# A bounded number of gathers in flight in place of a full drain on the gather engine

## The reference

```
x = x + _L0_conv_ref(_gn(x), W, b)                 # attention over pixels, squared-ReLU scores
x = x + _L1_conv_ref(_gn(x), offset_w, ...)        # deformable convolution, 9 taps
x = x + _L2_conv_ref(_gn(x), w_i2s, ...)           # diagonal LSTM, two directions
x = x + _L3_conv_ref(_gn(x), w_conv, w_p, ...)     # deformable convolution with adaptive reach
```

```
sampled = (hh*hw) * gather(y0, x0)   + (hh*lw) * gather(y0, x0+1)
        + (lh*hw) * gather(y0+1, x0) + (lh*lw) * gather(y0+1, x0+1)
out = einsum('nckhw,ock->nohw', sampled * mask, wk)
```

## Time and profile before

| What | Value |
|---|---|
| median of three runs | 12763.94 us |
| span of the profiled execution | 13258.5 us |
| POOL busy | 7518.9 us (57%) |
| PE busy | 7451.2 us (56%) |
| DVE busy | 6180.1 us (47%) |
| ACT busy | 4757.6 us (36%) |
| mean granted TensorE clock | 0.745 of full speed |
| first stage, first to last gather | 465.7 to 6534.7 us |
| last stage, first to last gather | 8067.3 to 13235.7 us |
| moved by DMA | 1280.23 MB, of them 925.30 MB by the gathers |

### The profile page before, as it was taken

The page is one execution under the profiler, slowest core; times in us unless marked ns, Lnnn a source line. Parts: engine busy times, 40 slices in busy tenths (PEclk is TensorE's granted clock), DMA queues, the critical chain, the costliest instruction groups (busy, mean ns, idle before and its releaser), DMA issues. The chain is left out here.

```text
span 13258.5 us, 114790 instructions
## 1 busy us (share of the span) xinstructions
PE 7451.2 (56%) x29878; PEld 2708.4 (20%) x29878; DVE 6180.1 (47%) x8631; ACT 4757.6 (36%) x7391; POOL 7518.9 (57%) x7857
## 2 busy tenths in 40 slices
PE   7786776778777676853289992333232323233332
PEld 2222222222222222221123321111111111111111
DVE  1344444444433444445456664454455445545444
ACT  7664554646555454641156661111111111111100
POOL 0375655657565564757500004777777767767776
PEclk9897887889888787876599995565565656555665
DMA  0232232223322222337633337343434343433332
GB/s 9 66 96 87 85 93 80 87 89 96 92 85 79 89 85 86 91 94 172 164 86 81 82 78 139 101 121 101 120 97 119 101 111 98 120 97 101 100 96 90
DMA packets 1169072, 1280.23 MB, mean 97 GB/s; under 512 B 795966, under 2 KB 924414, under 8 KB 1164670
## 3 DMA queue, kind: packets, MB, share of 16 engines
q0 software_dynamic: 338688, 925.30, 23.5%
q1 hardware_dynamic: 815710, 347.84, 11.1%
q10 hardware_dynamic: 14368, 3.21, 0.1%
HBM read 1080.00 MB, written 195.82 MB: 96 GB/s over the span
## 5 line engine op out<-in xcount | busy, mean ns | idle before, releaser
L423 POOL DMA_INDIRECT b_gathered<-table,b_iu x3528 | 3701.6, 1049 | 1929.9 <-issue 1013.0
L423 POOL DMA_INDIRECT d_gathered<-table,d_iu x3528 | 3705.2, 1050 | 1420.4 <-issue 1041.0
L526 PE MATMUL PS<-ident,d_sample 128*128 128x128 f32 (+1 forms) x1960 | 509.6, 424 | 2978.1 <-DVE d_sample L879 2090.9
L504 PE MATMUL PS<-b_key 64*128 64x448 f32 (+1 forms) x5600 | 1516.6, 622 | 448.9 <-ACT b_weights L665 300.1
L665 ACT ACTIVATE b_weights<-PS 128x896 f32<-128x896 f32 (+1 forms) x1400 | 1270.1, 907 | 1287.5 <-remote 882.8
L861 DVE TENSOR_TENSOR d_gathered<-d_gathered,PS 128x2304 f32<-128x2304 f32 x392 | 1000.9, 2553 | 1184.1 <-DMA d_gathered<-table,d_iu 1115.1
L514 PE MATMUL PS<-b_weights,b_values 128*64 128x448 f32 (+1 forms) x5600 | 1462.9, 603 | 123.1 <-issue 73.4
L668 ACT ACTIVATE b_weights<-b_weights 128x896 f32<-128x896 f32 (+1 forms) x1400 | 1332.3, 952 | 44.7
L674 ACT ACTIVATE d_sampleT<-PS 128x512 f32<-128x512 f32 x392 | 233.6, 596 | 2894.4 <-PE PS L526 2000.9
L526 PEld LDWEIGHTS PS<-ident,d_sample 128*128 128x128 f32 (+1 forms) x1960 | 336.0, 205 | 3130.8 <-issue 2721.1
L866 DVE TENSOR_TENSOR b_gathered<-b_gathered,PS 128x1152 f32<-128x1152 f32 x392 | 529.9, 1352 | 819.3 <-DMA b_gathered<-table,b_iu 802.6
(11 more groups left out here) (227 smaller groups left out, 9679.5 us busy)
## 6 DMA issues: line engine op xcount, KB each, us to landing
b_gathered<-table,b_iu POOLq DMA_INDIRECT x3528
d_gathered<-table,d_iu POOLq DMA_INDIRECT x3528
l_x_and_h<-xs SPq DMA_DIRECT2D x224, 224.0 KB, 3.9
hs<-l_hT SPq DMA_DIRECT2D x224, 224.0 KB, 2.8
d_h<-hs SPq DMA_DIRECT2D x32, 1554.0 KB
table<-b_table_rows SPq DMA_DIRECT2D x208, 128.0 KB, 2.0
table<-d_table_rows SPq DMA_DIRECT2D x208, 128.0 KB
xs<-b_key SPq DMA_DIRECT2D x14, 1568.0 KB
```

The source lines that it names most:

```text
L423: pool.indirect_dma_start(GB[:, g, k, :], None, tables[b], bass.IndirectOffsetOnAxis(ap=ix, axis=0)).then_inc(gathered[g], 16)
L504: mm = pe.matmul(PS[0:keys(k), 2 * (k % S_BUFS) + a, 0:CH], KEY[r, 0, k * P:k * P + keys(k)], KEY[r, 0, j * CH:(j + 1) * CH], start=True, ...
L526: mm = pe.transpose(PS[0:n, 5 + 2 * (s // 4), (s % 4) * P:(s % 4 + 1) * P], S[:, t % 2, s * P:s * P + n], K.ident[:, :])
```

## The change

The column, its memset and its semaphore go. Each gather now also carries a second semaphore, `described`, to which the gather engine adds one when it has finished the instruction itself, descriptors written and DMA started (the landing of the data is still told by `gathered`). Ahead of the first, fourth and seventh gather of a tile the engine waits until all but the four newest of the gathers issued so far have signalled. The count starts at nine, so that no wait is for zero or less.

```
+IN_FLIGHT = 4
...
-        DRAIN = sb("drain", [P, 1])
...
-        pool_drained = sm("pool_drained")
+        described = sm("described")
...
+            pool.sem_inc(described, TAPS)
...
                     for t in range(TPC):
                         g = t % G_BUFS
-                        pool.memset(DRAIN[:, :], 0.0).then_inc(pool_drained, 1)
-                        wait_apart(pool, pool_drained, c * TPC + t + 1)
                         wait_apart(pool, samples_ready, c * TPC + t + 1 - BACK[t] + TPC)
                         for k in range(TAPS):
+                            if k % 3 == 0:
+                                wait_apart(pool, described, (c * TPC + t) * TAPS + k + TAPS - IN_FLIGHT)
                             n = (j * TPC + t) * TAPS + k
                             ix = IU[b][:, n:n + 1]
                             pool.indirect_dma_start(GB[:, g, k, :], None, tables[b],
-                                                    bass.IndirectOffsetOnAxis(ap=ix, axis=0)).then_inc(gathered[g], 16)
+                                                    bass.IndirectOffsetOnAxis(ap=ix, axis=0),
+                                                    engine_sem=described).then_inc(gathered[g], 16)
```

## The result

The changed kernel takes 12073.2 us (12066.34 to 12086.47, four runs) against 12767.9 us before: the ratio is 0.9455, 95% interval 0.9444 to 0.9466. It is 695 us faster. The forecast was 12402 us, 362 less, with a range down to 12250; the direction was right and the size about half.

A forecast was written before the change was run, and what follows sets the result against it. The gather engine (POOL) was taken to set the last stage's pace, and the first's in part. Savings of 221 + 35 + 120 = 376 us, scaled by 0.963 to 362, gave 12764 - 362 = 12402 us, range 12250 to 12640.

The forecast's parts named there:

- The mechanism: Three new waits a tile cost nothing, hidden by four unfinished gathers (5 us of work); uncovered, up to 0.71 us each.
- The last round of the first stage: 49 tiles with no other engine near, where the removed drain saves 35 us.
- A: First stage: attention holds it, POOL's saving becomes longer waits for samples; 256 us saved, scaled 247, 12517 us; chance 0.12.
- B: End of each of 7056 gathers: the signal costs up to 0.12 us; 12966 us, slower; chance 0.08 near full price.
- C: Three waits a tile are not hidden, each costing 0.71 us as the drain did; 13542 us; chance 0.03.
- D: Tile's end: the 0.90 us stop stays with the first gather, only the memset's 0.12 goes; 12698 us; chance 0.06.
- The seven rounds beside attention: First stage, 343 tiles: 120 us saved, a little below the middle of 70 and 209, with 0 the floor.
- I scale all by it: Whole saving: 376 us of profile time times 12763.94 / 13258.5 = 0.963 gives 362 us without the profiler.
- The hand-backs of the last stage: Of 265 us saved there, 17 return as longer gathers and 27 as longer waits for samples, leaving 221.
- The 17: Last stage, first chunks of pairs: DMA engines hold the gathers, so half of 49 tiles' 35 us saving returns.
- Below zero I exclude: Second semaphore on each gather: its cost lies between nothing and 0.12 us, never a gain; taken as nothing.
- its best case: Whole kernel: 265 + 35 + 209 = 509 us saved, 490 scaled, 12274 us; about 12245 if PE keeps its higher clock.

## Why the prediction was right in kind and half in size

*Right.* The bound: all of the gain is in the gather engine's own time. The mechanism: waits kept behind unfinished gathers cost nothing, as the memset without a gap had shown, and the cover of four was more than enough, one does. The end of the tile: 1.01 us became 0.30. The last round of the first stage: 35 us forecast, and from first to last gather 645 and 616 us in undisturbed profiles, 31 of it from stops. The saving a tile was 0.69 us on average for 0.71, since some stops before were 0.95 and not 1.01. The seven waits of the first stage took back what the four tiles ahead of them saved: 270 (391 x 0.69) less 251, some 19 us. Rivals A, B, C and D are refuted: the first stage gave more than half of the gain, the signal has no price that shows, the waits are hidden, and no stop of 0.9 is left at a tile's end.

*The terms that failed.*

1. "The seven rounds beside attention ... I take 120." That step rested on the 49 waits of the earlier trace rows and the stops of ScalarE of the earlier trace rows, which were of one disturbed execution. Undisturbed, POOL sets the pace in these rounds too and waits for a sample only once in each, and the stops give 218 us in the seven rounds where 120 stood (251 in the whole stage, where 35 + 120 = 155 stood).

2. "I scale all by it, as I don't know where the profiler's time lies." The 480 us were no share of every microsecond: gathers and ordinary stops had the same lengths in both profiles, and the excess was irregular waits, most of it in the first stage. The factor 0.963 took 14 us off for nothing. The difference between span and runs, 3.9%, was in plain sight, and was a reason to distrust waits that came irregularly, not to scale.

3. The hand-backs of the last stage, "265 - 17 - 27 = 221": neither came. The idle time fell by 268 us, the one long wait for a sample grew from 11.0 to 12.5 us only, and the gathers became shorter, not longer. The 17 stood on a wrong reading of the earlier trace rows, that the DMA engines held POOL in a pair's first chunk. The same profile has two gathers there that make up nearly all of the 76.1 - 65.3 = 10.8 us, and both start inside an addition of VectorE with two SBUF operands, POOL first, then DVE:

```profile
9378.83 5.99 POOL L423 DMA_INDIRECT d_gathered<-table,d_iu  x1 [0.30 <-issue]
9385.13 5.55 POOL L423 DMA_INDIRECT d_gathered<-table,d_iu  x1 [0.30 <-issue]
```

```profile
9378.06 5.93 DVE L741 TENSOR_TENSOR d_x<-d_x,d_h 128x3136 f32<-128x3136 f32 x1 [10.85 <-DMA d_x<-x]
9384.02 5.82 DVE L744 TENSOR_TENSOR d_x<-d_x,d_h 128x3080 f32<-128x3080 f32 x1
```

They are 5.99 - 0.95 and 5.55 - 0.95, 9.6 us in all, too long. The sign of the collision that term 4 lacks stood in the rows that were blamed on the DMA engines.

4. "Below zero I exclude: nothing of the gather goes away." This was said of the signal and holds for it. But no term at all stood for the length of a gather, though the earlier trace rows showed a mean of 1.05 beside the usual 0.95. It moved by 76 + 108 = 184 us, a quarter of the whole gain. The lengthening was treated as a constant of 0.1 us, where it comes from gathers that start inside a VectorE operation with two SBUF operands (the additions, and in the first stage the right half of the weighing), and its price depends on how far into the operation they start.

In sum: 519 us from stops where 376 stood (and 362 after scaling), 184 from shorter gathers where nothing stood. The second put the time below the range: its best case had 509 us of stops before scaling, and with 519 us alone the kernel would have taken 12767.9 - 519 = 12249 us, the range's lower end. That the direction of the 184 was a gain is luck of the rhythm as far as the forecast goes: nothing in it says which way the gathers' length would move.

## What to carry to other kernels

An engine that waits for its own last instruction pays the way of the signal and the restart each time; here 0.47 to 0.71 us. Let it wait for an older one: here a single unfinished gather, longer than that way, hid three waits a tile. Before reading waits from a profile, hold its span against the timed runs; where they differ by more than the runs among themselves, take a second profile. Here the regular patterns (0.30 and 1.01) came back in it, and the irregular waits did not. And where an instruction's mean is above its usual length, ask what it collides with, since a change of rhythm moves the collisions.

## What the runs showed of the hardware

- A gather on GpSimd that starts inside a VectorE operation with two SBUF operands is lengthened by the rest of that operation less 0.13 us; one that starts inside an operation whose second operand is in PSUM keeps its 0.95 us, and so does one that was already running when the operation began. In the changed kernel a gather that started in one of a tile's operations took up to 2.1 us, one that started in the 5.94 us addition of `d_x` up to 6.7. Replacing one such operation a tile shortened the last stage's gathers by 195 us in the changed kernel (3658.6 to 3463.3).
- Two SBUF operands are not the only case. The gather that starts in L749 (`d_gp` from `d_x` and two columns, 128 x 3136 in 1.92 us) is lengthened by the same rule, by 1.28 us on average in six cases of before. What these operations have in common was not tried.
- VectorE is not held up in turn: its column addition took 1.35 to 1.36 us in nearly every tile of the changed kernel's last stage (1.42 at most), with a gather already running or without.
- Ahead of each gather stand 0.30 us in which the engine takes no other gather but does take a memset of 0.12 us (0.12 + 0.19 = 0.31).
- From the end of a gather that signals by itself to the start of the next that waits for it are 0.77 us; by way of a memset behind it, 1.01 us (0.95 in part of the tiles).
- The second semaphore on a gather costs nothing that 7056 of them would show (ratio 1.0003, 0.9994 to 1.0013).
- The issuing part of the engine runs ahead of the gathers: a wait for all but the four newest let go 5.3 us before the gather behind it started.
